# First two image pairs of a vision layer: the edge filter applied to the three colour planes instead of a grey picture

## The reference, cut to what matters

```python
w = jnp.asarray((0.2989, 0.587, 0.114))
gray = jnp.einsum('bchw,c->bhw', x, w)[:, None]
edges = conv_general_dilated(gray, scharr, window_strides=(1, 1), padding='SAME')
abs_edges = jnp.sqrt(jnp.square(edges))
edge = abs_edges.sum(axis=1) / 2
...
h = edge
h = h + attn(_layernorm(h))   # k, v, r projections, WKV scan, output projection
h = h + ffn(_layernorm(h))    # 8 experts, top-1 routing
```

## Time and profile before

| | us |
|---|---|
| median of 3 runs | 1179.91 (1176.8 to 1180.4) |
| the profiled execution, its own time | 1180.26 |
| its span, first to last instruction | 1178.5 |
| outside the span | 1.76 |

### The profile page before, as it was taken

One profiled execution on the slowest core, in us unless ns is written; L12 is line 12 of the kernel. 1 busy time (PEld: TensorE's weight loads), 2 busy tenths in 40 slices (PEclk: granted clock), 3 DMA queues, 4 the chain that ended last, 5 costly groups with the idle time before them and its releaser, 6 DMA issues.

```text
span 1178.5 us, 17076 instructions
## 1 busy us (share of the span) xinstructions
PE 1097.7 (93%) x5699; PEld 715.6 (61%) x5699; DVE 1033.9 (88%) x1869; ACT 880.0 (75%) x1407; POOL 171.4 (15%) x234
## 2 busy tenths in 40 slices
PE   0647899999999999999999999999999999999987
PEld 0223466666666666666666666666666666666665
DVE  2587799999999999999999999999999999999851
ACT  0366687888788878878888878888888788877641
POOL 4021110101111101011111111111111111110000
PEclk9878899999999999999999999999999999999999
DMA  7986667667766776677767676677676766760001
GB/s 190 204 161 110 103 149 158 141 123 153 152 140 135 156 153 146 123 141 155 144 136 146 154 153 134 124 163 148 131 147 146 163 136 123 152 99 22 19 18 36
DMA packets 163601, 155.70 MB, mean 132 GB/s; under 512 B 12444, under 2 KB 163570, under 8 KB 163570
## 3 DMA queue, kind: packets, MB, share of 16 engines
q1 hardware_dynamic: 125972, 119.77, 41.4%
q0 software_dynamic: 32640, 31.46, 21.6%
q10 hardware_dynamic: 4958, 4.07, 1.5%
HBM read 105.96 MB, written 65.03 MB: 145 GB/s over the span
## 4 chain that ended last, share of the span: by engine, by line
PE 88%; DMA 6%; SPq 2%; ACT 1%; DVE 1%; POOL 0%; issue 0%; ACTq 0%; POOLq 0%
PE bank L1135 26%; PE bank L1270 19%; PE bank L1198 15%; PE bank L1125 10%; PE bank L1174 9%; PE bank L1219 4%; DMA gray_dram<-planes 2%; DMA gray_dram<-rows_in 2%; DMA rows_in<-gray_dram 2%; PE bank L1248 2%; PE bank L1271 1%; PE bank L1210 1%; PE bank L1257 1%; SPq L346 1%; PE bank L1186 1%; DMA gray_dram<-in_x_dram 1%
## 5 line engine op out<-in xcount | busy, mean ns | idle before, releaser
L1270 PE MATMUL bank<-w_sb,hidden 128*128 128x256 f32 x1024 | 238.8, 380 | 1.9 <-ACT hidden L963 1.9
L1270 PEld LDWEIGHTS bank<-w_sb,hidden 128*128 128x128 f32 x1024 | 184.8, 191 | 30.1 <-ACT hidden L963 2.6
L1125 PE MATMUL bank<-rows_in,conv_w 102*32 102x512 f32 x1024 | 138.3, 641 | 47.9 <-DMA rows_in<-gray_dram 47.9
L1135 PE MATMUL bank<-mixed_r,w_r_t 128*128 128x512 f32 x256 | 127.4, 622 | 8.8 <-ACT v_sb L892 8.8
L1198 PE MATMUL bank<-normed_hi,w_hi 128*128 128x512 f32 x256 | 128.2, 501 | 3.2 <-DVE normed_lo L721 3.2
L1135 PE MATMUL bank<-mixed_v,w_v_t 128*128 128x512 f32 x256 | 122.0, 600 | 0.4 <-ACT edge L876 0.4
L1174 PE MATMUL bank<-w_o_t,rwkv 128*128 128x256 f32 x512 | 116.9, 382 | 0.3 <-DVE rwkv L695 0.3
L440 POOL TENSOR_TENSOR pool_turn<-pool_turn 128x1 f32<-128x1 f32 x30 | 5.5, 184 | 721.8 <-ACT planes L884 676.3
L1174 PEld LDWEIGHTS bank<-w_o_t,rwkv 128*128 128x128 f32 x512 | 98.2, 192 | 15.7 <-issue 1.1
L1198 PE MATMUL bank<-normed_lo,w_hi 128*128 128x512 f32 x256 | 101.4, 396 | 0.0
L1198 PE MATMUL bank<-normed_hi,w_lo 128*128 128x512 f32 x256 | 100.8, 394 | 0.0
(11 more groups left out here) (144 smaller groups left out, 2308.3 us busy)
## 6 DMA issues: line engine op xcount, KB each, us to landing
rows_in<-gray_dram SPq DMA_DIRECT2D x186, 256.0 KB
planes<-in_x_dram SPq DMA_DIRECT2D x124, 256.0 KB, 3.5
gray_dram<-planes POOLq DMA_DIRECT2D x120, 256.0 KB, 5.9
out_dram<-resid SPq DMA_DIRECT2D x64, 256.0 KB, 2.2
gray_dram<-in_x_dram SPq DMA_DIRECT2D x60, 256.0 KB, 5.1
rows_in<-gray_dram SPq DMA_DIRECT2D x124, 24.0 KB
rows_in<-gray_dram ACTq DMA_DIRECT2D x6, 256.0 KB
planes<-in_x_dram ACTq DMA_DIRECT2D x4, 256.0 KB, 7.3
```

The lines of the kernel that those rows point to most:

```text
L1125: ins = pe.matmul(bank[BANK_EDGE[n]][ROW_TILE * q:ROW_TILE * (q + 1), :], conv_w[0:TAPS, c, :], rows, start=True, stop=True)
L1135: ins = pe.matmul(ps[:, :], weights[:, kt, ct * P:(ct + 1) * P], part[:, 2 * kt:2 * kt + 2, :].rearrange("p i t -> p (i t)"), start=(kt == ...
L1270: pe.matmul(ps, hidden[:, m, i, rows], w2_sb[:, m, :], start=(m == 0), stop=False)
```

## The change

Pairs 0 and 1 no longer get a grey picture. `load_colors` brings rows of x straight to `rows_in`: red's 32 rows of a tile on partitions 0 to 31, green's on 32 to 63, blue's on 64 to 95, and the rows above and below, for three colours, on the 6 others. The grey weights are folded into three weight tiles `color_w`, one for each column shift. `convolve` makes each part of these two pairs with three accumulating products a tile: the unshifted one over 512 columns, and the two shifted ones over 2 x 255. From pair 2 on nothing changes in what is computed. DVE zeroes the rows outside the picture and builds `color_w` first, and builds `conv_w` ahead of step 3 (`setup_conv`). The zero border of `gray_dram` is written by two DMAs of ACT: the rows (4x2x257) and the columns (4x257x2, pieces of 8 bytes); SP waits for both before it loads pair 2's rows. `load_later_weights` moves from ahead of step 2 to ahead of step 3 on SP. POOL builds `taps` first and `mask_rows` last, and `s_built` comes earlier.

```diff
@@ helpers @@
-        def load_first(eng, i, half):
-
-            for plane, dst in enumerate((planes[i][:, 2 * half:2 * half + 2, 0, :],
-                                         planes[i][:, 2 * half:2 * half + 2, 1, :],
-                                         first_blue[i][:, 2 * half:2 * half + 2, :])):
-                src = x[2 * i:2 * i + 2, plane, half * P:(half + 1) * P, :]
-                eng.dma_start(dst, src.rearrange("n p w -> p n w")).then_inc(first_in[i][half], 16)
-
-        def store_first(eng, i, half):
-
-            dst = gray_dram[i, :, 1 + half * P:1 + (half + 1) * P, :].rearrange("i p w -> p i w")
-            eng.wait_ge(s_first_zeros, 1)
-            eng.wait_ge(s_first_gray, HALF * i + half + 1)
-            eng.dma_start(dst, first_gray[i][:, 2 * half:2 * half + 2, :]).then_inc(first_stored[i], 16)
+        def load_colors(eng, pair, i):
+
+            buf, base = pair % 2, (2 * pair + i) * NCOL * T * D
+            for color in range(NCOL):
+                src = bass.AP(x.tensor, base + color * T * D, [[D, ROW_TILE], [ROW_TILE * D, TILES], [1, D]])
+                eng.dma_start(rows_in[buf][ROW_TILE * color:ROW_TILE * (color + 1), :, i, :], src
+                              ).then_inc(rows_loaded[buf], 16)
+            if pair < 2:
+                eng.wait_ge(s_outside, 2 * pair + 2)
+            for k in range(2):
+                src = bass.AP(x.tensor, base + (ROW_TILE - 1 + k) * D,
+                              [[T * D, NCOL], [ROW_TILE * D, TILES - 1], [1, D]])
+                first = 3 * ROW_TILE + 3 * k
+                eng.dma_start(rows_in[buf][first:first + 3, 1 - k:TILES - k, i, :], src
+                              ).then_inc(rows_loaded[buf], 16)
@@ SP @@
-            load_first(sp, 0, 0)
-            load_first(sp, 1, 0)
-            store_first(sp, 0, 0)
-            sp.wait_ge(s_borders, 16)
-            sp.wait_ge(first_stored[0], 16 * HALF)
-            load_rows(sp, 0, 0)
-            store_first(sp, 1, 0)
+            load_colors(sp, 0, 0)
+            load_colors(sp, 1, 0)
             for src, dst in zip((Wk, Wv), w_raw):
                 sp.dma_start(dst, src.rearrange("(a p) c -> p a c", p=P)).then_inc(s_w_in, 16)
-            sp.wait_ge(first_stored[1], 16 * HALF)
-            load_rows(sp, 1, 0)
 
             def load_later_weights():
                 for ct in range(CH):
                     sp.dma_start(w1_raw[:, ct, :].rearrange("p (e h) -> p e h", e=E),
                                  W1[:, ct * P:(ct + 1) * P, :].rearrange("e p h -> p e h")).then_inc(s_w1_in, 16)
+                sp.wait_ge(s_cleared, CLEARED_B2)
...
-                    if at.is_step(2) or at.is_step(3):
-                        sp.wait_ge(s_first_gray, HALF * (at.u - 1))
...
+                    if at.is_step(FIRST + GRAY):
+                        sp.wait_ge(s_borders, 32)
...
-            run_steps(sp, step, {2: load_later_weights})
+            run_steps(sp, step, {3: load_later_weights})
@@ DVE @@
+            for b in range(2):
+                dve.memset(rows_in[b][3 * ROW_TILE:TAPS, 0, :, :], 0.0).then_inc(s_outside, 1)
+                dve.memset(rows_in[b][3 * ROW_TILE:TAPS, TILES - 1, :, :], 0.0).then_inc(s_outside, 1)
+            dve.memset(zero_pairs, 0.0).then_inc(s_zeros, 1)
+            for color in range(NCOL):
+                dve.memset(shade[ROW_TILE * color:ROW_TILE * (color + 1), :], GRAY_WEIGHTS[color])
+            for n in range(6):
+                dve.memset(shade[3 * ROW_TILE:TAPS - n, :], GRAY_WEIGHTS[2 - n % 3]).then_inc(s_shade, 1)
+                dve.wait_ge(s_shade, n + 1)
+
+            dve.wait_ge(s_scharr_all_in, 16)
+            done(dve.tensor_scalar(scharr_all[0:TAPS, :], scharr_all[0:TAPS, :], shade[0:TAPS, :], 0.5,
+                                   ALU.mult, ALU.mult))
             dve.wait_ge(s_cleared, CLEARED_TAPS)
             for di in range(3):
                 for c in range(2):
+                    weights = scharr_all[0:TAPS, 9 * c + 3 * di:9 * c + 3 * di + 3]
+                    ins = dve.tensor_tensor((color_w if di == 0 else color_part)[0:TAPS, c, :, :],
+                                            taps[0:TAPS, di, :].unsqueeze(1).to_broadcast([TAPS, 3, ROW_TILE]),
+                                            weights.unsqueeze(2).to_broadcast([TAPS, 3, ROW_TILE]), ALU.mult)
+                if di > 0:
+                    ins.then_inc(s_color_part, 1)
+                    dve.wait_ge(s_color_part, di)
+                    done(dve.tensor_tensor(color_w[0:TAPS, :, :, :], color_w[0:TAPS, :, :, :],
+                                           color_part[0:TAPS, :, :, :], ALU.add))
+
+            assert own[0] == SETUP_FIRST
+
...
@@ ACT @@
-            load_first(act, 0, 1)
+            act.dma_start(scharr_all[0:TAPS, :], bass.AP(scharr.tensor, 0, [[0, TAPS], [1, 18]])
+                          ).then_inc(s_scharr_all_in, 16)
+            load_colors(act, 0, 1)
+            load_colors(act, 1, 1)
...
-            act.wait_ge(s_first_zeros, 1)
-            act.dma_start(bass.AP(gray_dram.tensor, 0, [[IMAGE, 4], [(T + 1) * PITCH, 2], [1, PITCH]]),
-                          zero_rows.unsqueeze(1).to_broadcast([4, 2, PITCH])).then_inc(s_borders, 16)
-            store_first(act, 0, 1)
-            act.wait_ge(s_borders, 16)
-            act.wait_ge(first_stored[0], 16 * HALF)
-            load_rows(act, 0, 1)
-            store_first(act, 1, 1)
-            rows = [(ROW_W, w.rearrange("(r c) -> r c", c=P)), (ROW_U, u.rearrange("(r c) -> r c", c=P))]
...
+            act.wait_ge(s_zeros, 1)
+            act.dma_start(bass.AP(gray_dram.tensor, 0, [[IMAGE, 4], [(T + 1) * PITCH + 1, 2], [1, T + 1]]),
+                          zero_pairs[:, 0:T + 1].unsqueeze(1).to_broadcast([4, 2, T + 1])).then_inc(s_borders, 16)
+            act.dma_start(bass.AP(gray_dram.tensor, D + 1, [[IMAGE, 4], [PITCH, T + 1], [1, 2]]),
+                          zero_pairs.rearrange("p (t k) -> p t k", k=2),
+                          allow_slow_non_contiguous=True).then_inc(s_borders, 16)
@@ PE @@
-                for q in range(4):
-                    rows = rows_in[at.buf(EDGE)][0:TAPS, 4 * half + q, :, :].rearrange("p i w -> p (i w)")
-                    ins = pe.matmul(bank[BANK_EDGE[n]][ROW_TILE * q:ROW_TILE * (q + 1), :],
-                                    conv_w[0:TAPS, c, :], rows, start=True, stop=True)
+                rows = rows_in[at.buf(EDGE)][0:TAPS, 4 * half:4 * half + 4, :, :]
+                if at.has_later(EDGE):
+                    for q in range(4):
+                        ins = pe.matmul(bank[BANK_EDGE[n]][ROW_TILE * q:ROW_TILE * (q + 1), :],
+                                        conv_w[0:TAPS, c, :], rows[:, q, :, :].rearrange("p i w -> p (i w)"),
+                                        start=True, stop=True)
+                else:
+                    sums = pair_view(bank[BANK_EDGE[n]])
+                    for dj, to, of in ((1, 0, 0), (0, 1, 0), (2, 0, 1)):
+                        width = D - (dj != 1)
+                        for q in range(4):
+                            ins = pe.matmul(sums[ROW_TILE * q:ROW_TILE * (q + 1), :, to:to + width],
+                                            color_w[0:TAPS, c, dj, :], rows[:, q, :, of:of + width],
+                                            start=(dj == 1), stop=(dj == 2))
```

More of the change, by code:

```diff
@@ L384, in _ @@
         def _(pool):
[L385 to L393 removed]
             pool.memset(taps[:, :, :], 0.0).then_inc(s_cleared, 1)
[L395 removed]
+            pool.wait_ge(s_cleared, 1)
             for di in range(3):
@@ L522, in setup_first_layer @@
             def setup_first_layer():
+                setup_conv()
                 dve.wait_ge(s_w1_in, 32)
```

150 lines of the change are left out of this document (66 added, 84 removed).

## The result

The changed kernel takes 1165.54 us (median of 4 runs, 1163.15 to 1167.32), the kernel before 1180.16 beside it (1176.8 to 1180.49): a ratio of 0.9881, 95% interval 0.9852 to 0.991. That is 14.6 us less; 13.3 were forecast. The interval lies clear of 1.

The account below looks back on a forecast made before the run. PE, saturated from 123.9 us, bounds the kernel; only that start can move. Gains along the chain were 12.0 us at pair 0's filter end, 12.7 at the scaling, 13.3 at POOL: 1180.26 - 13.3 = 1167.0 us, range 1160 to 1178.

Parts of the forecast that it names:

- What bounds: PE is saturated from 123.9 us, a rigid block; the change can only move the time at which that starts.
- Part 1: Pair 0's rows load directly, issued at 0.8 us and taking the old reload's 13.7, so they arrive at 14.5.
- The bound of 16: Upper bound in us for pair 0's arrival, as pair 1's rows follow at once on all queues.
- the rival of fast rows: Pair 0's rows arrive at 10 instead of 14.5 us, giving 1162.5; chance 0.10.
- Part 2: Pair 0's filter: 8 slow and 16 fast groups of four records, 13.5 us, ending 12.0 us earlier.
- The rival's slow pace for all 24 fours: Pair 0's groups of four records all slow, +6.3 us; with pair 1's too, 1176; chance 0.18, shared with late ACT.
- Part 3: From pair 0's filter end to pair 1's filter: 8.8 us of unchanged work, so pair 1's starts at 36.8.
- Part 4: Pair 1's filter and ACT's scaling of pair 2: 7.3 us for 12 groups, scaling at 44.7, 12.7 us earlier.
- What is late next: The other path, pair 0's products K and WKV, ends at 70.0, 5.7 us ahead of pair 2's rows.
- ACT's issues: ACT computes only behind 27 DMA issues; free at 24 to 25 us, nothing lost.
- The late border: The column border's 1,028 pieces land at 87 us, delaying pair 2's rows by 11 us, giving 1191; chance 0.13.
- The sum: The whole kernel's time: 1180.26 less 13.3 us gives 1167.0.

Follow-up runs that it names:

- run again: The changed kernel, nothing edited, run again: 1165.9 us, ratio 0.9884 to the kernel before.
- the weights back: The changed kernel with SP again issuing W1, b2, Wo, Wg and W2 ahead of pair 2's planes: 1166.06 us, ratio 0.989.
- the order of the colours: The changed kernel with SP loading red, blue, green and ACT blue, red, green: 1167.7 us, ratio 0.9894.
- the borders ahead: The changed kernel with the two border DMAs ahead of the small filter weights' loads on ACT's queue: 1172.95 us, ratio 0.9957.

## Why the prediction was right, point by point

| step | forecast | measured |
|---|---|---|
| PE's first filter record | 14.5 | 15.84 |
| pair 0's filter takes | 13.5 | 13.51 |
| ACT's table load | before 25 | 21.33 |
| pair 1's filter starts | 36.8 | 38.19 |
| scaling of pair 2 | 44.7 | 46.20 |
| POOL's first turn | 46.7 | 48.34 |
| SP issues pair 2's rows | 62.5 | 63.22 |
| PE on pair 2 | 75.7 | 76.60 |
| step 5 | 110.6 | 110.85 |
| time | 1167.0 | 1165.54 |

**What bounds.** Right: the change acts by the moment at which PE becomes saturated, 13.05 us at step 5, and the steady part is the same to 0.01 us. "Rigid" was too strong for the rest: 2 us in step 5 and 1.4 in the draining steps differ between the two profiled executions, both by the clock, and two executions of the changed kernel differ by 2.3 in the same way.

**Part 1, the arrival.** The mechanism was right, the term was 1.3 us too small. The forecast took the old reload's 13.7 us, issue to start. The bound of 16 named the reason, pair 1's rows right behind; taking them away gave 2.5 us back, so they belonged in the value and not only in the bound. The 13.36 of pair 0 alone lies below 14.5 and far above the 10 of the rival of fast rows, because of the tail.

**Part 2, the filter.** The mechanism was right, slow fours first and then fast ones, and 13.51 meets 13.5. That it does so to 0.01 us is luck: there were some 5.7 us of slow pace where 6.6 were forecast, and the fast fours took 0.44 and not 0.43. In four other profiles with the same three products and the same place of the first filter (run again, the weights back, the order of the colours, the borders ahead) it took 13.06, 12.10, 12.26 and 12.39 us; pair 1's filter varied the other way, from 9.75 to 11.04 us. The bound for an all-fast filter, 10.3, was measured as 10.48. The rival's slow pace for all 24 fours did not come up in any profile.

**Part 3.** 8.84 us from the filter's end to pair 1's (29.35 to 38.19), 8.8 forecast. Only the experiments show how close another path lay: DVE's work on the weights ended at 37.1, a microsecond before.

**Part 4.** From pair 1's filter to the scaling 8.0 us against 7.9, with the clock back at about 42.5, 4.3 us into the filter, where 4.2 were forecast. (The sum takes 0.86 us for a slow four here and 0.82 in part 2, which moves it by some 0.1.) So the scaling is late by 1.5, 1.4 of it inherited, 1.3 from the arrival. Then 0.9 came back behind POOL: from its first turn to SP's rows took 14.9 us where it had taken 15.8 in the earlier trace rows, because POOL's second turn lasts 0.18 us and no longer 2.06, while its first accumulating DMA landed a microsecond more slowly (8.1 us from the first turn to the second, 7.1 before). That was no part of the sum.

**What is late next.** Right that the DMA chain still decides: PE waits 5.37 us for pair 2's rows. `copy_normed` of step 3 ends at 71.9 where 70.0 was forecast, so its slack is 4.7 us and not 5.7; product K began at 48.14 and not 46.6, with the whole chain.

**ACT's issues.** Right in its result, before 25 and at no cost; at 21.3 it came 3 us earlier than the value. A queue with much in it does hold its issuer: the three filter weights took 4.90 us to issue, and 1.47 when pair 1's rows had waited. The forecast left open whether the last, narrow DMA holds ACT itself; it doesn't (1.25 us). With five DMAs behind it, it costs 7 us (8.6 by the ratios).

**The late border.** It did not come: the queue of ACT carries small pieces from 24 to 34 us, 331, 292 and 416 of them in the last three windows of 2 us, together about as many as the border has. The last window, 32 to 34:

```profile
q10 hardware_dynamic: 416, 0.00, 11.7%
```

That is about 150 to 210 pieces a us, two to three times the 76 that the rival's price was made from, and it landed some 29 us before SP wanted it. How many engines carried it can't be read from this row.

**The sum.** At step 5 the forecast of 110.6 met 110.85 with opposite errors: 1.5 us late at the scaling, and then the 0.9 behind POOL and 0.7 in step 4 came back. The total, 14.6 against 13.3, is the difference of two medians whose executions differ by 3.7 and 4.2 us, of which 2.3 could be followed in two profiles, to the clock behind step 5, about which the sum says nothing. So the mechanism is confirmed by the places, and the closeness of the two totals is partly luck.

## What to carry to other kernels

In a kernel whose main engine is saturated from some moment on, a change in the filling stages is worth what it moves that moment, and work may be trebled there if it replaces a trip through memory on which the engine waited: here TensorE is busy 11 us more and the kernel takes 14.6 us less. Compare such places in the profiles and not only the times, since the clock behind them can move a time by 2 to 4 us. Sum such a change along the chain of first events (arrival, filter, scaling, accumulation, rows), look one path further each time, and count the loads that are issued right behind the one that is waited for. A wait that the profile shows need not be worth its length: taking away one of 3.76 us moved the rows' issue by 1.8, since the DMA behind it took longer in its new place.

## What the runs showed of the hardware

- A DMA of 1,028 pieces of 8 bytes was issued in 0.32 us and held the issue of the three small DMAs behind it for 18 us, and with it the engine's computing.
- PE began its first products at half pace even though the granted clock was recorded as 1.00 there. The pace doubled 5.7 us into pair 0's filter in the profiled changed kernel and about 5 us into the unused products. The granted clock came back 3.3 us into step 5 of the changed kernel, 9.8 in the same kernel run again, and 7.6 in the kernel before.
- In two executions of one kernel that alone moved everything behind step 5 by 2.3 us. In the draining steps a further stretch at 0.50 cost 1.4 us in the kernel before, and in the kernel with 60 unused products they took 4.2 us more than in the changed one.
- An accumulating DMA that took 7.0 us from the start of its issue until POOL's next turn (60.16 to 67.15) took 10.4 (56.54 to 66.89) when it was issued earlier, into full DMA engines.
- Two queues that wrote different partitions moved no more in a window of 2 us than two that wrote the same (202 and 243 GB/s).
- Once TensorE is saturated its steps repeat exactly: 28 of them took 937.41 us in both kernels, at the granted clock 1.00 but for short stretches at their ends.
